# Key-value products of the last layer's recurrence moved from VectorE to GpSimd, with the values projected once and spread by transfers

## What is computed

```python
r = xr @ Wr; k = xk @ Wk; v = xv @ Wv; g = silu(xg @ Wg)
w_log = -exp(time_decay + tanh(xw @ decay_w1) @ decay_w2)
def fwd_step(S, inp):                      # S: (B, H, K, K)
    rt, kt, vt, wt = inp
    S = exp(wt)[..., None] * S + kt[..., None] * vt[..., None, :]
    return S, einsum('bhk,bhkv->bhv', rt, S)
def bwd_step(S, inp):
    rt, kt, vt, wt = inp
    y = einsum('bhk,bhkv->bhv', rt, S)
    S = exp(wt)[..., None] * (S + kt[..., None] * vt[..., None, :])
    return S, y
y = (y_f + y_b) * sigmoid(dx @ gate_w + gate_b)
# group norm over each head, * ln_w + ln_b, * g, @ Wo
```

## Time and profile before

| | us |
|---|---|
| median of 3 runs | 2316.47 |
| the profiled execution's own time | 2314.24 |
| its span (first to last instruction) | 2312.5 |
| last scan's end (start 2268.12 + 2.27) | 2270.4 |
| first scan's start | 1997.2 |
| busy in the span: PE / DVE / ACT / POOL | 2062.4 / 1623.5 / 1283.3 / 947.6 |

### The profile page before, as it was taken

How to read it: one execution, slowest core, us unless ns; L and a number is a source line. 1 busy time by engine, 2 the same in 40 slices (tenths; PEclk the granted TensorE clock), 3 DMA queues, 4 the chain that set the end, 5 groups by cost and what they waited for, 6 DMA issues and landing times. The chain is left out here.

```text
span 2312.5 us, 56820 instructions
## 1 busy us (share of the span) xinstructions
PE 2062.4 (89%) x22888; PEld 1391.5 (60%) x22888; DVE 1623.5 (70%) x4129; ACT 1283.3 (55%) x2560; POOL 947.6 (41%) x1176
## 2 busy tenths in 40 slices
PE   4679998998999999999999796899999986889886
PEld 2448887996888887888887664344433333334233
DVE  7666664775666676667665563899898936698895
ACT  2247775565777777777776242267676763323323
POOL 2037776664678744665443032111111100154462
PEclk8789999999999999999999797699999997999998
DMA  6311113104011100000000063011111101000000
GB/s 180 106 64 38 39 38 97 50 29 149 21 39 19 35 3 20 2 21 3 3 2 2 16 205 106 16 43 49 38 37 38 40 4 38 0 0 9 0 9 19
DMA packets 77925, 94.14 MB, mean 41 GB/s; under 512 B 10145, under 2 KB 56242, under 8 KB 76002
## 3 DMA queue, kind: packets, MB, share of 16 engines
q1 hardware_dynamic: 64178, 77.23, 11.1%
q0 software_dynamic: 13488, 13.28, 2.9%
HBM read 54.55 MB, written 35.53 MB: 39 GB/s over the span
## 5 line engine op out<-in xcount | busy, mean ns | idle before, releaser
L1166 DVE TENSOR_REDUCE a_parts<-a_S 128x1 f32<-128x512 f32 (+1 forms) x576 | 363.0, 684 | 29.0 <-PE a_S L1050 22.7
L1137 ACT ACTIVATE WA<-a_E 128x1024 f32<-128x1024 f32 (+1 forms) x320 | 283.1, 940 | 117.9 <-PE a_E L1078 58.8
L1042 PE MATMUL a_S<-a_KS,a_QS 54*128 54x512 bf16 (+3 forms) x768 | 189.6, 348 | 31.0 <-DVE a_parts L1166 18.4
L463 POOL TENSOR_SCALAR WA<-WA,a1b_rinv 128x1024 f32<-128x1024 f32 (+3 forms) x192 | 142.5, 761 | 181.8 <-DVE a1b_rinv L802 181.6
L463 POOL TENSOR_SCALAR XR<-XR,a1b_rinv 128x768 f32<-128x768 f32 (+3 forms) x192 | 141.7, 752 | 118.9 <-DVE a1b_rinv L802 118.4
L618 PE MATMUL a1b_O<-a1b_PT,WA 128*64 128x128 f32 x3072 | 189.0, 276 | 0.0
L618 PEld LDWEIGHTS a1b_O<-a1b_PT,WA 128*64 128x64 f32 x3072 | 165.8, 137 | 6.5
L583 PE MATMUL a1b_B<-a1b_Kf,a1b_Qf 64*128 64x512 f32 (+2 forms) x768 | 156.2, 481 | 8.5 <-issue 4.6
L1042 PEld LDWEIGHTS a_S<-a_KS,a_QS 54*128 54x128 bf16 x768 | 58.7, 95 | 172.5 <-DVE a_parts L1166 136.0
L1090 PE MATMUL a_O<-WA,V 128*9 128x512 f32 (+3 forms) x1536 | 154.2, 489 | 0.1
L714 ACT ACTIVATE WA<-WA,a1b_nmax 128x1024 f32<-128x1024 f32 (+3 forms) x192 | 150.4, 792 | 1.3 <-DVE a1b_nmax L784 1.3
(11 more groups left out here) (533 smaller groups left out, 5890.9 us busy)
## 6 DMA issues: line engine op xcount, KB each, us to landing
WA<-in_w SPq DMA_DIRECT2D x8, 1024.0 KB, 9.0
a_QS<-qstack SPq DMA_DIRECT2D x32, 216.0 KB
a_KS<-kstack SPq DMA_DIRECT2D x32, 216.0 KB
a1b_tb<-tab SPq DMA_DIRECT2D x12, 512.0 KB
qstack<-f_parts SPq DMA_DIRECT2D x24, 256.0 KB
kstack<-f_parts SPq DMA_DIRECT2D x24, 256.0 KB
f_slots<-f1r_zrows SPq DMA_DIRECT2D x9, 516.0 KB
f1t_xs<-f_slots SPq DMA_DIRECT2D x9, 516.0 KB, 7.3
```

The source lines that it names most:

```text
L463: pool.tensor_scalar(v, v, rinv[:, e, u, part:part + 1], 1.0, ALU.mult, ALU.mult).then_inc(n_sb, 1)
L1042: ins = pe.matmul(pS[(at + half) % SB][:, lo:lo + n], QS[s][ROW[half], pair, i * P:(i + 1) * P], KS[s][ROW[half], pair, block * P:block * ...
L1137: act.activation(PT[q % NP][:, :, 0:w], pE[q % 2][:, :, 0:w], ACT.Exp).then_inc(e_sb, 1)
L1166: dve.tensor_reduce(peak, pS[at % SB][:, :].rearrange("p (c k) -> p c k", c=n), AX.X, ALU.max)\
```

## The change

- The values are projected once a batch, without repetition: a new kind of product, `v`, for each half batch, with every eighth column of `Wv8` (128 columns of 128 different value channels, ordered by v). ACT copies it to `vfull` in SBUF.
- SP writes `vfull` (128 x 1024) to a DRAM tensor `vrows`, and reads it back for each step: the 16 rows of value channel v, each repeated over its head's 8 key rows by the transfer's pattern, into one of three SBUF tiles `spread` (512 KB each; two of them, and `vfull`, are laid over mdx, mxr and mxk of the channel mixing, idle during the recurrence).
- POOL makes `kv = spread * k` into one of two SBUF tiles (`weigh`), one step ahead of the scans, and does so ahead of the sum and the product of each step. `Ss` is gone: the sum is written to `Sr[s]`, and multiplied in place.
- DVE's product L2567 is gone; both scans now read `dec` and `kv` from SBUF. PE's `values` is gone.

```diff
-    pV = kv = [ph.ps(f"V{i}", (P, T)) for i in range(2)]
+    pV = [ph.ps(f"V{i}", (P, T)) for i in range(2)]
+    NK, NV = 2, 3
+    kv = tile("kv", True)
...
+    vfull = flat[2]
+    spread = [tile("spread"), flat[0], flat[1]]
...
+    vrows = nc.dram_tensor("vrows", [B, P, T], F32).ap()
...
-    FIRST = ("t5a", "t5b", "gate", "m_w", "m_k", "d1", "m_v", "d2", "m_r", "k", "m_g", "r", "g")
-    NEXT = {0: ("t5a", "t5b", "gate"), 1: ("m_w",), 2: ("d1", "m_k"), 3: ("d2", "m_v"), 4: ("k", "m_r"), 5: ("r", "m_g"), 6: ("g",)}
+    FIRST = ("t5a", "t5b", "gate", "m_w", "m_k", "d1", "m_v", "d2", "v", "m_r", "k", "m_g", "r", "g")
+    NEXT = {0: ("t5a", "t5b", "gate"), 1: ("m_w",), 2: ("d1", "m_k"), 3: ("d2", "m_v"), 4: ("v", "k", "m_r"), 5: ("r", "m_g"), 6: ("g",)}
...
+            def write(b):
+                sp.wait_ge(emptied["v"], 2 * b + 2)
+                sp.dma_start(vrows[b, :, :], vfull[:, :]).then_inc(v_out, 16)
+
+            def read(n):
+                b, v = divmod(n, HK)
+                if n >= NV:
+                    sp.wait_ge(kv_sb, n - NV + 1)
+                elif n:
+                    sp.wait_ge((l_mixed, l_rk)[n - 1], EARLY)
+                if v == 0:
+                    sp.wait_ge(v_out, 16 * (b + 1))
+                src = bass.AP(vrows.tensor, (b * P + v * 16) * T, [[T, 16], [0, HK], [1, T]])
+                sp.dma_start(spread[n % NV][:, :], src).then_inc(spread_in[n % NV], 16)
...
+            def weigh(n):
+                if n >= NS:
+                    return
+                b, v = divmod(n, HK)
+                if v == 0:
+                    pool.wait_ge(emptied["k"], 2 * b + 2)
+                pool.wait_ge(spread_in[n % NV], 16 * (n // NV + 1))
+                if n >= NK:
+                    pool.wait_ge(scanned, n - NK + 1)
+                elif n == 0:
+                    pool.wait_ge(l_delta, EARLY - 1)
+                pool.tensor_tensor(kv[n % NK][:, :], spread[n % NV][:, :], k[b % 2][:, :], ALU.mult).then_inc(kv_sb, 1)
+
+            weigh(0)
+            weigh(1)
             for b in range(B):
                 for v in range(HK):
                     n, s = b * HK + v, v % 2
+                    if n:
+                        weigh(n + 1)
                     if v == 0:
                         pool.wait_ge(emptied["r"], 2 * b + 2)
                     if n >= 2:
                         pool.wait_ge(y_ps, n - 1)
                     pool.wait_ge(scanned, n + 1)
-                    if n:
-                        pool.wait_ge(sr_sb, n)
-                    pool.tensor_tensor(Ss[:, :], Sf[s][:, :], Sb[:, s, 1:T + 1], ALU.add).then_inc(sum_sb, 1)
+                    pool.tensor_tensor(Sr[s][:, :], Sf[s][:, :], Sb[:, s, 1:T + 1], ALU.add).then_inc(sum_sb, 1)
                     pool.wait_ge(sum_sb, n + 1)
-                    pool.tensor_tensor(Sr[s][:, :], Ss[:, :], r[b % 2][:, :], ALU.mult).then_inc(sr_sb, 1)
+                    pool.tensor_tensor(Sr[s][:, :], Sr[s][:, :], r[b % 2][:, :], ALU.mult).then_inc(sr_sb, 1)
...
+                elif kind == "v":
+                    pe.wait_ge(xv_sb, count)
+                    ins = pe.matmul(out[:, :], w["Wv8"][:, ::HK], xv[b % 2][:, cut], start=True, stop=True)
...
-                    dve.wait_ge(v_ps, n + 1)
                     if v == 0:
-                        dve.wait_ge(emptied["k"], 2 * b + 2)
                         dve.wait_ge(dec_sb, b + 1)
-                    dve.tensor_tensor(kv[s][:, :], pV[s][:, :], k[b % 2][:, :], ALU.mult).then_inc(kv_ps, 1)
                     if n >= 2:
                         dve.wait_ge(sum_sb, n - 1)
-                    dve.wait_ge(kv_ps, n + 1)
-                    dve.tensor_tensor_scan(Sf[s][:, :], dec[b % 2][:, :], kv[s][:, :], 0.0, ALU.mult, ALU.add)
-                    dve.tensor_tensor_scan(Sb[:, s, T - 1::-1], kv[s][:, ::-1], dec[b % 2][:, ::-1], 0.0,
+                    dve.wait_ge(kv_sb, n + 1)
+                    dve.tensor_tensor_scan(Sf[s][:, :], dec[b % 2][:, :], kv[n % NK][:, :], 0.0, ALU.mult, ALU.add)
+                    dve.tensor_tensor_scan(Sb[:, s, T - 1::-1], kv[n % NK][:, ::-1], dec[b % 2][:, ::-1], 0.0,
                                            ALU.add, ALU.mult).then_inc(scanned, 1)
```

More of the change, by code:

```diff
@@ L2131, in wkv @@
         ph.sem(n) for n in ("ldx", "lmixed", "lrk", "lrelu", "lk2", "lsig", "lv", "ldelta", "ltr", "lx"))
-    stored = ph.sem("stored")
+    stored, v_out = ph.sem("stored"), ph.sem("vout")
+    spread_in = [ph.sem(f"spreadin{i}") for i in range(NV)]
+    vrows = nc.dram_tensor("vrows", [B, P, T], F32).ap()
     rows_out = out.rearrange("(n p) d -> p n d", p=P)
@@ L2136, in wkv @@
     dx1, dx2, xv1, ln_sb, de_sb, yc_sb = (ph.sem(n) for n in ("dx1", "dx2", "xv1", "lnsb", "desb", "ycsb"))
[L2137 to L2139 removed]
+    kv_sb, scanned, sum_sb, sr_sb, y_ps, c_ps = (
+        ph.sem(n) for n in ("kvsb", "scanned", "sumsb", "srsb", "yps", "cps"))
+    KINDS = ("t5a", "t5b", "gate", "m_w", "m_k", "d1", "m_v", "v", "d2", "m_r", "k", "m_g", "r", "g", "cen", "var", "out")
     emptied = {kind: ph.sem("e" + kind.replace("_", "")) for kind in KINDS}
@@ L2174, in store @@
                 sp.dma_start(rows_out[:, c * CT:(c + n) * CT, :], X[:, c * CT:(c + n) * CT, :]).then_inc(stored, 16)
[L2176 to L2179, removed]
+            def write(b):
[11 more added lines that the diff above has]
+                sp.dma_start(spread[n % NV][:, :], src).then_inc(spread_in[n % NV], 16)
+            write(0)
+            for b in range(B):
+                for v in range(HK):
+                    if v == 6 and b + 1 < B:
+                        write(b + 1)
+                    read(b * HK + v)
+                    if v == 7 and b == 1:
+                        sp.wait_ge(l_x, EARLY)
+                    if v == 7 and 1 <= b <= 2:
+                        sp.wait_ge(emptied["out"], 2 * b)
+                        store(2 * b - 2, 2)
+            for slot in range(NV):
+                sp.wait_ge(spread_in[slot], 16 * len(range(slot, NS, NV)))
+            sp.wait_ge(v_out, 16 * B)
             sp.wait_ge(emptied["out"], 6)
@@ L2254, in product @@
                 ins.then_inc(c_ps, 1)
[L2256 to L2266, removed]
             def add(n):
@@ L2322, in _ @@
             both("d2", 0)
+            both("v", 0)
             first(3)
@@ L2382, in evacuate @@
                         ins = act.activation(dec[s][:, cut], src[:, :], ACT.Exp, bias=w["time_decay"])
+                    elif kind == "v":
+                        if b:
+                            act.wait_ge(v_out, 16 * b)
+                        ins = act.copy(vfull[:, cut], src[:, :])
                     elif kind == "k":
@@ L2452, in _ @@
                     decay(b + 1)
-                    for kind in ("k", "r", "g"):
+                    for kind in ("v", "k", "r", "g"):
                         evacuate(kind, b + 1)
```

12 lines of the change are left out of this document (6 added, 6 removed).

## The result

The changed kernel takes 2397.17 us (median of 4 runs, 2395.58 to 2399.57) against 2316.43 before (4 runs, 2313.53 to 2316.59). The ratio is 1.0357, 95% interval 1.0344 to 1.037: 81 us slower. Forecast were 2404 and a range of 2385 to 2434. The profiled execution took 2395.89 us, its span is 2394.1.

A forecast was written before the change was run, and what follows sets the result against it. DVE's own list of work was taken as the bound. Shared-way use 355.3 plus PE 3 made the stretch 358.3 against 273.2: +85.1; end +2.4; on 2314.24 that gave 2401.7, with the median 2.2 above: 2404, range 2385 to 2434.

The forecast's parts named there:

- The likeliest case: In the recurrence, scans with two SBUF operands and POOL operations go one after the other: 2404 us, chance 0.80.
- Rival 1: In the recurrence, a scan does not take the shared way: 2278 to 2302 us, about 2290, chance 0.13.
- rival 2: The shared way is held for only part of a scan, or by one of the two: about 2336 us, chance 0.03.
- rival 4: In the recurrence, each step waits for its transfer's read: 2430 us, chance 0.04 together with Rival 3.
- Rival 3: PE becomes the bound through the chain from begin to the mixes: 2420 us, chance 0.04 together with rival 4.
- a plain step on the shared way: Three POOL operations and two scans of one recurrence step in turn, less handovers: 10.9 us, 10.76 to 11.04.
- shared way in use, first to last scan: Steps plus DVE's other two-operand work, 366.8 us, less POOL operations outside the stretch: 355.3 us.
- shared way idle there: Between first and last scan, 1 us a batch for waits on PE: 3 us, bounds 0 and 12.
- start of the first scan: Write, read and two kv products after the copy of v: about 1998 against 1997.20, counted 0, bounds -4 and +6.
- behind the last scan: At the kernel's end, step 30's product stands after the last scan, ahead of the last sum: +2.4 us.
- the first of the two orders: In a plain step the engines alternate: kv product, sum, scan, product, scan, 10.76 us.
- DVE's present idle: In Rival 1's price, DVE's idle time in the recurrence, some 28 us, is added to its 207.5 busy.

The follow-up runs named there:

- e1: The changed kernel with the decay written by ACT to idle PSUM tiles, so each scan has one operand in PSUM: 2320.45 us, ratio 1.0026.
- e2: The kernel before with DVE's kv product written to SBUF instead of PSUM, so both scans have two SBUF operands: 2352.38 us, ratio 1.016.
- e4: The changed kernel with the decay written twice, the forward scan reading it from PSUM, the backward scan from SBUF: 2353.45 us, ratio 1.0164.
- e3: The changed kernel with only the first write and first three reads of spread values, later steps reusing those tiles: 2398.19 us, ratio 1.036.
- e6: e1 with DVE's addition for the mixed values left to PE, and kv products in five buffers, up to three steps ahead: 2317.34 us, ratio 0.9998.
- e8b: e6 with four last-batch kv products on DVE, and GpSimd's kv products after a batch's first step held until begin is over: 2298.06 us, ratio 0.9932.
- e10b: e8b with the wait one operation earlier, so GpSimd's product of a batch's first step also waits for begin: 2294.34 us, ratio 0.9913.
- e9b: The kernel before with one added wait: GpSimd's product of a batch's first step waits until DVE has finished begin: 2303.8 us, ratio 0.9958.

## Why the prediction was right

The likeliest case came in, and for the reason given: a scan with two SBUF operands and a POOL operation go one after the other. e1 takes the loss away and leaves POOL's third operation and the transfers; e2 brings it about without them; e4 gives a little over half. Rival 1 is out by the scans' means, rival 2 by the plain step, in which both scans wait and hold, rival 4 by e3. Rival 3, PE as the bound, is out by the overlap: the times in which POOL worked or DVE had an instruction with two SBUF operands, laid over one another, cover 354.6 of the 359.7 us between the scans, so waits for PE can have cost 5.2 at most. The Trainium skill, SBUF — State Buffer, Who interferes with whom, has the general rule for two SBUF inputs and a list of operations that leaves the scan out; by these runs the scan belongs to the rule.

Term by term the sum was less right than its total:

| step of the prediction | foretold | measured |
|---|---|---|
| a plain step on the shared way | 10.9 (10.76 to 11.04) | 10.52 |
| shared way in use, first to last scan | 355.3 | 354.6 |
| shared way idle there | 3 (0 to 12) | 5.2 |
| stretch from first to last scan | 358.3 | 359.7 (1992.41 to 2352.14) |
| start of the first scan | 1997.2, bounds -4, +6 | 1992.41, -4.8, outside the bounds |
| behind the last scan | +2.4 | -0.1 (42.0 against 42.1) |
| sum against the profiled span | +87.5 | +81.6 |

- *A step.* The engines alternate as in the first of the two orders. The handover hides more than 0.14 where POOL multiplies behind a scan: the product ends 2.13 after it, where alone it takes 2.35, so 0.22, and the kv product ends 2.14 after its scan. And POOL's sum ends 1.95 after its kv product, where I had put a gap on top of 2.00. Yet over the whole stretch the shared way was in use for as long as foretold. So what was too much in the plain steps was too little in the others, where DVE's other work comes in and the two alternate less; how it divides among them was not separated.
- *PE.* The cost put on PE was nearly right. The shared way was idle for 5.2 us in all; 1.4 and 1.9 of these are two gaps at the first mix of a batch, which DVE still waited for or was making (it has a PSUM operand) when POOL had run out of work. DVE waited there for 17.3 us in all, and POOL's backlog covered nearly all of it, as foretold.
- *The windows.* I read the windows of rows 1 as eight steps each. They hold 9, 8, 8 and 7, so "some 85 us" for the last was the price of a step too many: it took 77.1. No term of the sum hangs on it.
- *The start.* Everything up to the mixed values came 1.7 us earlier than in the kernel before (L2531 from 1971.46, L2489 from 1973.15), by the earlier end of the phases ahead. ACT's copy of the values was over at 1982.6 against my 1984, SP's write went out at 1982.66, the reads from 1985.29 on, the first kv product started at 1989.92, and the first scan started before the second kv product was made. From the copy to the first scan it was 9.8 us, not 13.7: one kv product fewer stood ahead (2.4), and write and read took 7.3 together, not 9.0.
- *The end.* I had put the product of step 30 behind the last scan. In the alternating order it runs between the last two scans, so nothing is added; my own first order said so, and the sum did not follow it.

Rival 1's price, 2278 to 2302, was e1's forecast too (2275 to 2302), and e1 took 2320. The step that failed there is that "DVE's present idle" of 28 us would stay: it was 69.3. 17.2 of these are waits for kv; the waits for the mixes rose from 17.3 to 32.9, those of `gated` from 2.8 to 10.6, as POOL's last product of a batch comes later with a third operation, and 2.9 are a new wait for ACT at the first `begin`. Removing the waits for kv shortened the stretch by only 2.4 (e6), keeping POOL out of `begin`'s way by 12.8 and 7.4 more (e8b, e10b). With both, the stretch is 253.7, inside the 235 to 260 of rival 1. But the same remedy takes 6.7 off the kernel before, so these waits were not all e1's own, and how much of its excess each kind made was not separated.

## What to carry to other kernels

Before work moves to GpSimd, or a tile from PSUM to SBUF, count per VectorE operation how many operands lie in SBUF; here those with two passed one at a time with GpSimd's, and the time of the loop was the sum of both lists, less 0.05 to 0.22 us at each handover. If a PSUM tile is idle, one operand put there buys the overlap (77 us here, for no instruction more: ACT writes its result there instead). Where some such meetings can't be avoided, choose which: a GpSimd operation held back until a short chain-starting VectorE operation was through took 6.7 us off the recurrence of a kernel that had looked tuned. And before a small difference between totals is explained, see in the traces whether it lies where the edit acts.

## What was not expected of the hardware

- A wait of 2 us on DVE cost 3.3 at the first mix of the second batch (kernel before against e9b). Between them are PE's matrix instructions. Four of L2224 took 2.70 us in the kernel before, with a granted clock of 0.73 from 2080 to 2086, after PE had stood idle for 2.25 and 1.14 us. The same four (L2226) took 1.90 in e9b, with 1.00 from 2074 to 2080.

```profile
2081.60 2.70 PE L2224 MATMUL a_C<-a_x,WA 128*32 128x512 f32 x4
```

```profile
2076.10 1.90 PE L2226 MATMUL a_C<-a_x,WA 128*32 128x512 f32 x4
```

  At the turn to the third batch the same four took 3.62 and 1.90 us, with granted clocks of 0.50 and 1.00, its two levels of 1.2 and 2.4 GHz, and in the first batch it was the other way round, 1.90 and 2.87. So which stretch of the chain runs at the lower clock changed with the timing, and the gain from one and the same wait was 0.9, 3.3 and 4.7 us on the three ways.

- The granted clock was 0.92 to 0.98 in the windows before, 0.79 to 0.83 in the first three after and 0.68 in the last, where PE is busy for 31 of 77 us. It did not set the time of the changed kernel, as the shared way was idle for only 5.2 us.
